# Recurrent stage on one core: another order of the third block on DVE and PE, and four squares made by ACT

## The reference

```python
x_prev = concatenate([x[:, :1], x[:, :-1]], axis=1)
k, v, r = split(_layernorm(x, g1, b1) @ W_tm, 3)
k = k * tmk + x_prev * (1 - tmk)
v = v * tmv + x_prev * (1 - tmv)
r = sigmoid(r * tmr + x_prev * (1 - tmr))
y = _wkv(time_decay, time_first, k, v)      # recurrence over the tokens
x = x + r * y
xp = concatenate([x[:, -1:], x[:, :-1]], axis=1)
xn = _layernorm(x, g2, b2)
kk = (xn @ W_cm) * cmk4 + xp4 * (1 - cmk4)  # 128 -> 512 channels
rr = sigmoid(xn * cmr + xp * (1 - cmr))
vv = square(relu(kk)) @ W_cp                # 512 -> 128 channels
x = x + rr * vv
```

## Time and profile before

| what | value |
|---|---|
| median of 3 runs | 717.51 us (716.87 to 718.19) |
| the profiled execution, its own time | 717.23 us |
| its span, first to last instruction | 715.3 us |
| PE busy | 673.5 us, 94% |
| DVE busy | 570.0 us, 80% |
| ACT busy | 417.0 us, 58% |
| POOL busy | 324.5 us, 45% |
| granted TensorE clock, mean | 0.994 |

### The profile page before, as it was taken

How to read it: one execution, slowest core, us unless ns; L and a number is a source line. 1 busy time by engine, 2 the same in 40 slices (tenths; PEclk the granted TensorE clock), 3 DMA queues, 4 the chain that set the end, 5 groups by cost and what they waited for, 6 DMA issues and landing times. The chain is left out here.

```text
span 715.3 us, 12389 instructions
## 1 busy us (share of the span) xinstructions
PE 673.5 (94%) x4100; PEld 501.9 (70%) x4100; DVE 570.0 (80%) x1310; ACT 417.0 (58%) x755; POOL 324.5 (45%) x404
## 2 busy tenths in 40 slices
PE   7899998697899999999999988999999998999997
PEld 5677774543467777777778676777777775777785
DVE  5899978889979888987989867676766676879774
ACT  4657676885246555555656666555565654555554
POOL 2668873101227766456757543220413200545463
PEclk9999999999999999999999999999999999999999
DMA  6636420000014233212313000000000000323231
GB/s 173 200 102 181 161 84 1 0 1 1 1 47 133 71 108 90 90 59 75 104 58 92 30 1 1 2 3 1 2 1 0 0 2 1 120 74 119 61 119 44
DMA packets 34329, 43.16 MB, mean 60 GB/s; under 512 B 5216, under 2 KB 17504, under 8 KB 34272
## 3 DMA queue, kind: packets, MB, share of 16 engines
q1 hardware_dynamic: 34272, 42.46, 19.3%
HBM read 41.13 MB, written 1.31 MB: 59 GB/s over the span
## 5 line engine op out<-in xcount | busy, mean ns | idle before, releaser
L697 POOL TENSOR_TENSOR p_prod<-p_p,p_gate_row 128x512 f32<-128x512 f32 x128 | 204.0, 1605 | 105.7 <-DVE p_p L504 62.3
L384 ACT ACTIVATE p_sil<-p_ps_a 128x512 f32<-128x512 f32 x176 | 105.3, 598 | 131.9 <-PE p_ps_a L100 127.0
L509 DVE TENSOR_TENSOR p_hlo<-p_prod,p_hhi 128x512 fp32r<-128x512 f32 x176 | 149.5, 851 | 0.3 <-ACT p_hhi L393 0.2
L504 DVE TENSOR_TENSOR p_p<-p_sil,p_ps_b 128x512 f32<-128x512 f32 x128 | 87.0, 680 | 51.8 <-ACT p_sil L384 37.3
L393 ACT CAST p_hhi<-p_prod 128x512 fp32r<-128x512 f32 x176 | 108.1, 615 | 21.8 <-POOL p_prod L697 21.8
L98 PE MATMUL p_ps_a<-xt_hi,w_uphi 128*128 128x512 f32 x176 | 74.2, 422 | 0.0
L98 PE MATMUL p_ps_acc<-p_hhi,w_downhi 128*128 128x512 f32 x176 | 71.0, 404 | 1.2 <-DVE p_hlo L509 1.0
L98 PE MATMUL p_ps_b<-xt_hi,w_uphi 128*128 128x512 f32 x176 | 71.1, 404 | 0.1
L100 PE MATMUL p_ps_a<-xt_hi,w_uplo 128*128 128x512 f32 x176 | 70.1, 398 | 0.0
L99 PE MATMUL p_ps_a<-xt_lo,w_uphi 128*128 128x512 f32 x176 | 70.1, 398 | 0.0
L100 PE MATMUL p_ps_b<-xt_hi,w_uplo 128*128 128x512 f32 x176 | 69.9, 397 | 0.0
(11 more groups left out here) (356 smaller groups left out, 1421.4 us busy)
## 6 DMA issues: line engine op xcount, KB each, us to landing
p_gate_row<-gate_rows SPq DMA_DIRECT2D x128, 256.0 KB, 3.3
w_rawbuf<-in_L_ffn_fc_w_dram SPq DMA_DIRECT2D x3, 512.0 KB, 6.2
w_rawbuf<-in_L_ffn_w_dram SPq DMA_DIRECT2D x3, 512.0 KB, 5.7
out_dram<-x SPq DMA_DIRECT2D x4, 256.0 KB, 3.6
w_rawbuf<-in_L_ffn_shared_w_dram SPq DMA_DIRECT2D x3, 256.0 KB, 3.9
x<-in_L_attn_x_dram SPq DMA_DIRECT2D x2, 256.0 KB, 3.8
x<-in_L_attn_x_dram SPq DMA_DIRECT2D x1, 512.0 KB, 8.5
mb_xraw<-in_L_attn_W_B_dram SPq DMA_DIRECT2D x1, 512.0 KB, 5.0
```

Of the source, the lines that this page charges most:

```text
L384: nc.scalar.activation(sil[:, u % 2], ps_a[:, u % 2], ACT.Silu).then_inc(c["sil"].sem, 1)
L504: nc.vector.tensor_tensor(dst, sil[:, u % 2], ps_b[:, u % 2], ALU.mult).then_inc(c["p1"].sem, 1)
L509: nc.vector.tensor_tensor(hlo[:, u % R], prod[:, u % R], hhi[:, u % R].bitcast(F32), ALU.subtract).then_inc(c["hlo"].sem, 1)
L697: G.tensor_tensor(prod[:, u % R], p1[:, u % 2], gate_row[:, e % ROWS], ALU.mult).then_inc(c["prod"].sem, 1)
```

## The change

Three edits. First, DVE and PE get another order for block 2's chain end, block 3's chain and the channel mixes of blocks 1 and 2. Second, the squares of the quarters 8, 9, 12 and 14 leave DVE; ACT makes each of them in two instructions, `Relu` in place on `kx` and `Square` into `sq`, with a semaphore between, and DVE's `square(13)` and `square(15)` wait for ACT's `square(12)` and `square(14)`, so that they are counted in order. Third, ACT takes `factors(3)` ahead of `shifted_k(2)` and `shifted_r(2)`.

```diff
 # PE
             turn_out(0)
             grow(6)
+            turn_x2(2)
+            shrink(4)
             grow(7)
-            shrink(4)
-            turn_x2(2)
             shrink(5)
             shrink(6)
+            turn_z2(2)
             shrink(7)
-            turn_z2(2)
+            grow(8)
+            grow(9)
             turn_out(1)
-            grow(8)
             turn_x2(3)
-            grow(9)
+            shrink(8)
+            shrink(9)
             grow(10)
-            shrink(8)
             grow(11)
-            shrink(9)
             turn_z2(3)
 # ACT
+            def square(n):
+                act.wait_ge(c["r_kx"].sem, c["r_kx"].at(n + 1))
+                act.wait_ge(c["r_sq"].sem, c["r_sq"].at(n))
+                act.wait_ge(c["r_vv"].sem, c["r_vv"].at(n - 1))
+                A(kx[n % 2][:], kx[n % 2][:], ACT.Relu).then_inc(c["r_rect"].sem, 1)
+                act.wait_ge(c["r_rect"].sem, c["r_rect"].at(RECT.index(n) + 1))
+                A(sq[n % 2][:], kx[n % 2][:], ACT.Square).then_inc(c["r_sq"].sem, 1)
...
             thresh(3)
+            factors(3)
             shifted_k(2)
             shifted_r(2)
-            factors(3)
             tokens2(2)
             take_z2(2)
+            square(8)
+            square(9)
             tokens2(3)
             shifted_k(3)
             take_z2(3)
             shifted_r(3)
             receive2(2)
             receive2(3)
+            square(12)
+            square(14)
 # DVE
             def square(n):
                 dve.wait_ge(c["r_kx"].sem, c["r_kx"].at(n + 1))
+                if n - 1 in RECT:
+                    dve.wait_ge(c["r_sq"].sem, c["r_sq"].at(n))
...
             output(2)
+            received(2)
+            residual(2)
+            add_out(0)
+            lead2(3)
+            parts2(3)
+            measure2(2)
+            wrap(2)
             shift(5)
             square(5)
             shift(6)
-            received(2)
-            add_out(0)
-            residual(2)
-            lead2(3)
-            wrap(2)
-            parts2(3)
-            measure2(2)
+            numerator(3)
+            numerators(3)
             square(6)
             shift(7)
+            apart(3)
             square(7)
-            numerator(3)
-            numerators(3)
+            blend(3)
+            shift(8)
             gated(1)
-            apart(3)
-            blend(3)
             output(3)
             received(3)
             residual(3)
-            shift(8)
-            square(8)
-            measure2(3)
             add_out(1)
             shift(9)
+            measure2(3)
             shift(10)
-            square(9)
             gate_in(2)
             square(10)
             wrap(3)
...
             shift(12)
-            square(12)
             shift(13)
             square(13)
             add_out(2)
             shift(14)
             shift(15)
-            square(14)
             square(15)
+RECT = (8, 9, 12, 14)
```

More of the change, by code:

```diff
@@ L1593, in rwkv_phase @@
     per = {"r_kk": 4, "r_kx": 4, "r_sq": 4, "r_vv": 4, "r_c1": 2, "r_c3": 2}
+    c["r_rect"].base += len(RECT)
     once = {"r_prep": 1, "r_om": 1, "r_uw": 1, "r_vec": 1}
@@ L2439, in program @@
         counts.update({n: Count(sem(n)) for n in RWKV_SEMS})
+        counts["r_rect"] = Count(sem("r_rect"))
         counts.update({n: counts[spent] if spent else Count(sem(n)) for n, spent in zip(MAMBA_SEMS, SPENT)})
```

## The result

| | before | changed |
|---|---|---|
| median, 4 runs each | 717.73 us (716.87 to 718.19) | 724.12 us (723.72 to 725.20) |
| profiled execution, span | 715.3 us | 723.3 us |
| its mean granted clock | 0.994 | 0.985 |

The medians differ by 6.4 us, a factor of 1.0089; the ratio on record is 1.0078, with a 95% interval of 1.0061 to 1.0095, which is 4.4 to 6.8 us. Slower by 3.4 to 3.8 us was forecast (721.1 us, 719.3 to 722.9). The direction was right, the size was not.

What follows compares the result with a forecast made beforehand. DVE was taken to bound the stretch from 165 to 202 us. Added waits of 6.70 us less 2.88 us of relief gave +3.8 on 717.23 us, so 721.0, median 0.3 above; 721.1 us was predicted, range 719.3 to 722.9.

Steps and rivals of the forecast that it cites:

- The waits and the stage: Block 2 and 3 stage, to the last add_out: new DVE waits of 7.85 us, net +3.8 us.
- ACT's pair: Relu then Square on ACT for each moved square: 1.27 us, against 0.69 for the one DVE instruction.
- The profiled execution took 717.23 us, so 721.0: Whole kernel: the stage's +3.8 us put on the old profiled execution's time; the median lies 0.3 us above it.
- the base: Whole kernel before: profiled execution of 717.23 us, with the median of the runs 0.3 us above.
- Everything behind the stage moves along: Stages behind the changed one: the next opens 3.8 us later, since it opens behind these steps and PE fills it.
- The first rival, the clock: PE gaps between shrink(4) and grow(7) bring the half clock into this stage: 721.6 to 722.7 us, chance 0.17.
- C: Theory tested in the experiments: the new order's gaps on PE call up half-clock episodes; no chance given.
- The third rival: In this stage the waits do not come and DVE's 2.88 us are gained: 714.3 us, chance 0.05.
- the last sum: Whole kernel: profiled 717.23 us gives 721.0, the median lies 0.3 above it, and 721.1 us is predicted.

Runs made afterwards that it cites:

- the control: The kernel before, unchanged, run again under its own name beside the null kernel and the changed kernel on one chip: 718.68 us, ratio 1.0006.
- the null kernel: The kernel before with eight one-column activations added where ACT is idle and one more semaphore, PE's and DVE's orders unchanged: 719.00 us, ratio 1.0013.
- three moves on PE: The changed kernel with turn_z2(2) ahead of shrink(6), grow(8) ahead of shrink(7) and grow(10) ahead of turn_x2(3) in PE's list: 721.26 us.
- The squares alone: The kernel before, with its old PE and DVE order, but squares 8, 9, 12 and 14 made by ACT in two steps: 719.02 us, ratio 1.0007.
- the order alone: The changed kernel's new order of the three engines, but with all sixteen squares on DVE: 724.91 us, ratio 1.0085.
- two swaps: The changed kernel with gated(1) ahead of shift(8) on DVE and grow(10) ahead of turn_x2(3) on PE: 722.52 us.
- both laid-out ones: The changed kernel with its three lists reordered by a step-by-step layout: 724.13 us; again with the last add_out behind head_measure(1) and head_low(0): 719.33 us.
- the kernel with fillers: The changed kernel with 36 identity transposes added on PE in four gaps of the stage: 722.35 us.

## Why the prediction was right in direction and too small

**The waits and the stage: right.** The changed kernel's stage was 44.04, 44.04 and 44.03 us in three profiles, the old one's 40.22 in three (the first, the control and the null kernel). +3.82 against +3.8, and over 16 and 64 executions +4.0 us (3.5 to 4.4) at an equal clock. `shift(8)`, `residual(3)` and `shift(10)` waited for what was named, and PE's order is their cause for the two `shift`s: three moves on PE took these waits to 0.2 us.

**ACT's pair: right.** 1.29 us. The squares alone are worth nothing in the old order, as that run shows, and about 0.9 us in the new one (+4.9 without them, +4.0 with them). In neither is the move a loss.

**The step that failed: "The profiled execution took 717.23 us, so 721.0".** It carried the half-clock episodes of that one execution, mean clock 0.994, over to the changed kernel, and let the clock into the range only by a fall in this stage, at 0.17 and up to +1.6 us. The four executions that made the result had clocks of 0.985, 0.989, 0.987 and 0.992, mean 0.9883. Only one clock of the kernel before is on record for that comparison, so the fit's constants have to stand in for the rest. Measured was 3.0 us above the forecast. By the fit 1.9 us of that are the clock (5.7 x 0.324), 0.8 the base (718.1 us for the kernel before at 0.994, where the forecast built on 721.1 - 3.8 = 717.3), 0.2 the change itself (4.0 against 3.8), and 0.1 is left. The forecast said "Everything behind the stage moves along", and gave the clock of those stages no term. The measured terms are +2.79 us behind the stage and +1.39 ahead of it in that one execution, and the table of the same program's two profiles shows that such terms are the half clock's. The later executions of the same program came out at medians of 722.80 and 721.92 us, inside the range, with mean clocks of 0.9920 and 0.9917. So the miss was in part the draw of four executions. Whether it was drawn by execution or by chip stays open: the chip of the first four isn't on record.

**The first rival, the clock, had the right thing at the wrong place.** No profile of the changed kernel shows the half clock between 165 and 207 us, although the idle time that the rival named is there (2.21 us ahead of `grow(7)`, 2.3 laid out). Of the profiles of other reordered stages, four had an episode in it (the order alone, two swaps, both laid-out ones) and two had none; of the five with the old order none had. The clocks say the same: 56 executions with some new order of this stage (the kernel with fillers left out) have a mean of 0.9898, 106 with the old order 0.9920, a difference of 0.0021 with a standard error of 0.0005. That speaks for C in such orders as a group, but the kernels differ in more than one thing, and I do not call it shown. Whether this change's order lowers the mean clock (0.9909 against 0.9923) stays open: a difference of 0.0013 is 0.4 us, and single executions of one kernel differ by ten times as much.

**The third rival** (DVE's relief is gained) failed where it was said to be decided: `grow(8)` and `grow(10)` were not ready. **The base** was too low as well: the median of the kernel before is 718.34 us over 64 executions, not 717.51. And the last sum does not close: 717.23 + 3.8 + 0.3 is 721.3, and 721.1 was written, which took the forecast 0.2 us further off.

## What to carry to other kernels

Where three engines hand work to each other with no slack, write the new order out with start-to-start durations from the trace before judging it: here that gave each of seven waits to 0.12 us. The layout must run to the first instruction of the next stage, not to the last one of this. Then ask what the execution at hand drew of the clock, and compare at an equal granted clock, or over a dozen executions, before a difference under 1% is put down to an edit.

## What the runs showed of the hardware

The same program's mean granted clock goes from 0.984 to 0.997 between executions, and its time with it, 0.32 us for each 0.001: 716.3 to 722.1 us for one unchanged kernel. In the profiles of this kernel and its variants an episode follows some microseconds of thin work on PE: in the changed kernel it was busy for 1.90 us of four ahead of the one at 127 us, 0.70 of two ahead of 141, 2.76 of six ahead of 421. Whether one follows is not settled by the work there: the kernel before had the same 1.90 us of four and the same 2.10 us of idle time ahead of the same instruction, and kept the full clock. What one costs depends on who waits for PE: 0.91 us at 605 us, 2.21 at 421 us for one twice as long. The Trainium skill (TensorE: Matmul & The Clock Gate, "HAM oscillation — how this bites in real kernels") describes such falls behind idle time on PE. These runs agree in that, and add that in one and the same program the places that are hit differ from execution to execution: 127, 141, 421 and 605 us in one profile of the changed kernel, none of them in the second, only the last, at 602 us, in the third.
